# A graph attention layer: query and x rows from one product, and biases and the carried row added by VectorE

## The reference

```
q = (x @ Wq + bq); k = (x @ Wk + bk); v = (x @ Wv + bv)      # 6250 x 128, 8 heads of 16
scores = sum(q[dst] * k[src], per head) * 16**-0.5 + (edge_attr_64 @ We + be)
max_s = segment_max(scores, dst)
e = exp(scores - max_s[dst])
denom = segment_sum(e, dst) + 1e-10
probs = e / denom[dst]
agg = segment_sum(probs * v[src], dst)
out = layernorm(x + agg @ Wo + bo)                            # no scale, no shift, eps 1e-5
```

## Time and profile before

| | us |
|---|---|
| runs | 2404.39, 2408.98, 2410.76 |
| median | 2408.98 |
| the profiled execution | 2400.68 |
| its span | 2398.6 |
| PE busy | 1449.8 |
| DVE busy | 1493.1 |
| ACT busy | 526.8 |
| POOL busy | 1496.5 |

### The profile page before, as it was taken

One profiled execution on the slowest core, in us unless ns is written; L12 is line 12 of the kernel. 1 busy time (PEld: TensorE's weight loads), 2 busy tenths in 40 slices (PEclk: granted clock), 3 DMA queues, 4 the chain that ended last, 5 costly groups with the idle time before them and its releaser, 6 DMA issues.

```text
span 2398.6 us, 23254 instructions
## 1 busy us (share of the span) xinstructions
PE 1449.8 (60%) x5480; PEld 979.4 (41%) x5480; DVE 1493.1 (62%) x3591; ACT 526.8 (22%) x1868; POOL 1496.5 (62%) x1572
## 2 busy tenths in 40 slices
PE   5454576656575666565655656565756565656566
PEld 4333353434343444343433434343434343434344
DVE  3365676657566666565666657565666666657666
ACT  0121221212122222222221222122222222222211
POOL 4745546666666666666666666666666666666661
PEclk7666777867677767777787777787877677777786
DMA  6643444545455445454545455454555454545440
GB/s 230 194 111 112 111 133 145 143 144 144 134 153 151 134 125 162 124 162 128 159 131 159 126 152 135 143 145 137 150 147 140 140 146 126 162 126 161 125 126 24
DMA packets 123029, 335.73 MB, mean 140 GB/s; under 512 B 47360, under 2 KB 55301, under 8 KB 115853
## 3 DMA queue, kind: packets, MB, share of 16 engines
q0 software_dynamic: 74624, 203.26, 30.1%
q1 hardware_dynamic: 45520, 124.28, 18.7%
q10 hardware_dynamic: 2748, 6.69, 0.7%
HBM read 323.82 MB, written 10.29 MB: 139 GB/s over the span
## 4 chain that ended last, share of the span: by engine, by line
POOL 32%; another core or an unknown queue 21%; issue 19%; PE 17%; DVE 9%; ACT 2%; DMA 1%; ACTq 0%; DVEq 0%
POOL kv_buf L487 32%; PE ps_a L1191 5%; PE ps_q L1156 4%; DVE prod L787 2%; DVE wv L819 2%; PE ps_t L1156 2%; PE ps_e L1168 1%; DVE score L797 1%; PE ps_a L1234 1%; DVE x_first L807 1%; ACT x_first L559 1%; PE ps_s L1213 1%; DMA kv_buf<-kv_table,src_i 1%; PE ps_s L1219 0%
## 5 line engine op out<-in xcount | busy, mean ns | idle before, releaser
L487 POOL DMA_INDIRECT kv_buf<-kv_table,src_i x1536 | 1468.9, 956 | 842.2 <-issue 437.9
L1191 PE MATMUL ps_a<-wv,x_first 128*128 128x272 f32 x1564 | 571.8, 500 | 325.3 <-ACT wv L605 188.5
L1191 PEld LDWEIGHTS ps_a<-wv,x_first 128*128 128x128 f32 x1564 | 362.3, 242 | 497.1 <-issue 212.1
L787 DVE TENSOR_TENSOR prod<-ps_q,kv_buf 128x512 f32<-128x512 f32 x262 | 179.9, 686 | 472.2 <-remote 296.2
L1156 PE MATMUL ps_q<-q_blk,x_first 128*128 128x256 f32 x1046 | 354.7, 472 | 22.6 <-issue 22.6
L797 DVE TENSOR_REDUCE score<-prod 128x32 f32<-128x512 f32 (+1 forms) x392 | 267.3, 682 | 7.9 <-issue 0.2
L819 DVE TENSOR_TENSOR wv<-kv_buf,ps_w 128x512 f32<-128x512 f32 (+1 forms) x392 | 266.0, 678 | 1.6 <-ACT keep L597 0.2
L1156 PEld LDWEIGHTS ps_q<-q_blk,x_first 128*128 128x128 f32 x1046 | 234.6, 239 | 79.1 <-issue 40.7
L787 DVE TENSOR_TENSOR prod<-ps_t,kv_buf 128x512 f32<-128x512 f32 (+1 forms) x130 | 89.1, 685 | 225.8 <-remote 128.4
L559 ACT ACTIVATE x_first<-dst_bc,neg_node 128x256 f32<-128x256 int32 (+1 forms) x392 | 197.0, 503 | 47.8 <-DMA dst_bc<-in_dst_row 30.4
L568 ACT ACTIVATE x_first<-x_first 128x256 f32<-128x256 f32 (+1 forms) x392 | 157.8, 403 | 215.8 <-remote 193.4
(11 more groups left out here) (140 smaller groups left out, 1550.3 us busy)
## 6 DMA issues: line engine op xcount, KB each, us to landing
edge_f<-in_edge_blk SPq DMA_DIRECT2D x55, 1024.0 KB
dst_bc<-in_dst_row SPq DMA_DIRECT2D x108, 448.0 KB
kv_buf<-kv_table,src_i POOLq DMA_INDIRECT x1536
kv_table<-kv_buf ACTq DMA_DIRECT2D x12, 512.0 KB, 2.7
xt_blk<-in_x_t SPq DMA_DIRECT2D x114, 32.0 KB
out<-y_out SPq DMA_DIRECT2D x114, 32.0 KB
kv_buf<-in_x_perm SPq DMA_DIRECT2D x5, 512.0 KB, 4.2
edge_f<-in_edge_blk SPq DMA_DIRECT2D x2, 512.0 KB
```

The costliest lines, as they stand in the source:

```text
L487: pool.indirect_dma_start(kv_buf[:, b % NBUF, t, :], None, kv_table, bass.IndirectOffsetOnAxis(ap=src_i[:, column:column + 1], axis=0)).th ...
L787: dve.tensor_tensor(prod[:, q % 2, 0:n * D].rearrange("p (t d) -> p t d", d=D), ps_q[q % SPREADS][:, 0:n * D].rearrange("p (t d) -> p t d" ...
L1191: one = pe.matmul(sums(b), edge_hots[:, q % EHOT, k * P:(k + 1) * P], wv[:, q % WVBUF, 2 * k:2 * k + 2, :].rearrange("p j w -> p (j w)"), ...
```

## The change

1. The one-row product of the carried row (`sum_carry`) is removed. After `copy_halves` has copied the two halves, DVE adds the carried row to row 0 of the copy, reading both from PSUM and `carried`. `copy_halves` now waits for PE's sum itself (`s_summed`), then for its own copies and for `s_carried`; `scale_carry` waits for `s_halves` in place of `s_carrysum`.
2. `project_q` issues one product of 256 columns: x with [Wq scaled, identity] (`w_qx`). ACT's `copy_q` is removed. DVE's `add_bias` adds the biases: two operations of 64x128 write the queries, one of 128x128 writes x + bo into a new buffer `x_res` (7 blocks deep).
3. `finish_rows` issues the product with Wo alone. ACT's `copy_projected` is removed; DVE's `add_rows` adds the product and `x_res` into `y_in`.
4. `xt_blk` has 3 buffers, not 7, and its load waits for the queries (`s_newq`), not for `finish_rows`.
5. At the start DVE builds `w_qx` (a scaling and a copy of the identity), PE spreads the two biases over all partitions with two one-row products, and DVE copies them. The first three blocks' `add_bias` stands on DVE ahead of the slots; the three `copy_q` stood on ACT.

The core of the diff:

```diff
+            def add_bias(b):
+                dve.wait_ge(s_newq, b + 1)
+                if b >= QBUF:
+                    dve.wait_ge(s_byedge, FIRST[b - QBUF + 1])
+                if b >= RBUF:
+                    dve.wait_ge(s_yin, b - RBUF + 1)
+                for j in range(2):
+                    own = slice(j * W, (j + 1) * W)
+                    dve.tensor_tensor(q_blk[own, b % QBUF, j * D:(j + 1) * D], new_qx[own, 0:D], bias_qo[own, 0:D], ALU.add)
+                dve.tensor_tensor(x_res[:, b % RBUF, :], new_qx[:, D:2 * D], bias_qo[:, D:2 * D], ALU.add).then_inc(s_qcopied, 1)
+
+            def add_rows(b):
+                dve.wait_ge(s_wo, b + 1)
+                if b >= 1:
+                    dve.wait_ge(s_normal, b)
+                dve.tensor_tensor(y_in[:, :], projected(b), x_res[:, b % RBUF, :], ALU.add).then_inc(s_yin, 1)
...
             def copy_halves(b):
-                dve.wait_ge(s_carrysum, b + 1)
+                dve.wait_ge(s_summed, FIRST[b + 1])
...
-                one.then_inc(s_halves, 1)
+                one.then_inc(s_copiedhalves, 1)
+                dve.wait_ge(s_copiedhalves, b + 1)
+                if b >= 1:
+                    dve.wait_ge(s_carried, b)
+                dve.tensor_tensor(sums_sb[0:1, b % 2, :], half_sums(b, 0)[0:1, :], carried[:, :], ALU.add).then_inc(s_halves, 1)
...
+                    if chain(v, 6) is not None and chain(v, 6) + QBUF < NB:
+                        add_bias(chain(v, 6) + QBUF)
+                    if at_node(v, 5) is not None:
+                        add_rows(at_node(v, 5))
...
-                pe.matmul(sums(b)[:, 0:WV], ident[0:1, :], carried[:, :], start=False, stop=True).then_inc(s_carrysum, 1)
...
-                pe.matmul(new_q, ones[0:1, :], bias_row[:, 0:D], start=True, stop=False)
-                pe.matmul(new_q, xt_blk[:, b % XBUF, :], w_qkv[:, 0:D], start=False, stop=True).then_inc(s_newq, 1)
+                pe.matmul(new_qx, xt_blk[:, b % XBUF, :], w_qx[:, :], start=True, stop=True).then_inc(s_newq, 1)
...
-                pe.matmul(projected(b), ones[0:1, :], bias_row[:, QKV:QKV + D], start=True, stop=False)
-                pe.matmul(projected(b), xt_blk[:, b % XBUF, :], ident[:, :], start=False, stop=False)
-                pe.matmul(projected(b), agg_t[:, :], w_o[:, :], start=False, stop=True).then_inc(s_wo, 1)
+                pe.matmul(projected(b), agg_t[:, :], w_o[:, :], start=True, stop=True).then_inc(s_wo, 1)
```

More of the change, by code:

```diff
@@ L275, in graph_attention @@
         s_found = sem("s_found")
-        FOUND = numbered("spread", "falls")
+        FOUND = numbered("spread", "bias qo", "falls")
         s_spread = sem("s_spread")
@@ L577, in copy_terms @@
                                ).then_inc(s_termscopied, 1)
-            def copy_q(b):
-                act.wait_ge(s_newq, b + 1)
-                if b >= QBUF:
-                    act.wait_ge(s_byedge, FIRST[b - QBUF + 1])
-                act.copy(q_blk[0:W, b % QBUF, 0:D], new_q[0:W, :])
-                act.copy(q_blk[W:P, b % QBUF, D:2 * D], new_q[W:P, :]).then_inc(s_qcopied, 1)
             def exponentials(b):
@@ L613, in copy_turned @@
                 act.copy(agg_t[:, :], turned(b)).then_inc(s_aggcopied, 1)
-            def copy_projected(b):
-                act.wait_ge(s_wo, b + 1)
-                if b >= 1:
-                    act.wait_ge(s_normal, b)
-                act.copy(y_in[:, :], projected(b)).then_inc(s_yin, 1)
             def inverse_deviation(b):
@@ L628, in _ @@
             with act.If(general == 0):
-                for b in range(min(QBUF, NB)):
-                    copy_q(b)
                 act.wait_ge(s_node, NODE["of blocks"])
@@ L638, in _ @@
                         exponentials(chain(v, 4))
-                    if chain(v, 6) is not None and chain(v, 6) + QBUF < NB:
-                        copy_q(chain(v, 6) + QBUF)
                     if at_node(v, 4) is not None:
                         copy_turned(at_node(v, 4))
-                    if at_node(v, 5) is not None:
-                        copy_projected(at_node(v, 5))
                     if step_in(v - SLOT - LAG) is not None:
@@ L961, in _ @@
             with dve.If(general == 0):
+                dve.wait_ge(s_const, CONST["bias qo"])
+                for b in range(min(QBUF, NB)):
+                    add_bias(b)
                 for v in SLOTS:
@@ L1115, in _ @@
             pe.matmul(step_ps[:, 0:1], ones[0:1, :], step_f[:, 0:1], start=True, stop=True).then_inc(s_found, 1)
+            pe.wait_ge(s_const, CONST["scaled"])
+            pe.matmul(spread_qo[:, 0:D], ones[0:1, :], bias_row[:, 0:D], start=True, stop=True)
+            pe.matmul(spread_qo[:, D:2 * D], ones[0:1, :], bias_row[:, QKV:QKV + D], start=True, stop=True).then_inc(s_found, 1)
             def turn_first(g):
@@ L1265, in _ @@
                         sum_step(v)
-                    if at_node(v, 0) is not None:
-                        sum_carry(at_node(v, 0))
                     if chain(v, 1) is not None:
@@ L1283, in _ @@
                     pe.matmul(ps_w[:, 0:D], ones[0:1, :], bias_row[:, 0:D], start=True, stop=False)
-                    pe.matmul(ps_w[:, 0:D], xt_blk[:, 0, :], w_qkv[:, 0:D], start=False, stop=True).then_inc(e_pe, 1)
+                    pe.matmul(ps_w[:, 0:D], xt_blk[:, 0, :], w_qx[:, 0:D], start=False, stop=True).then_inc(e_pe, 1)
                     after(pe, "pe", e_act, b * len(EACT) + EACT["q copied"])
```

29 lines of the change are left out of this document (17 added, 12 removed).

## The result

| | us |
|---|---|
| before, median of 20 | 2401.8 |
| changed kernel, median of 20 | 2413.32 (2403.1 to 2431.36) |
| ratio of the two, 95% interval | 1.0049 (1.0034 to 1.0064) |
| changed kernel, the profiled execution | 2418.86, span 2416.9 |

The change made the kernel about 0.5% slower. As a change I forecast +1 us; it was +11.5.

The account below looks back on a forecast made before the run. The prediction took a queue draining gathers at some 1.4 us each as the bound. Start +3, steady blocks +2 and end -4 gave +1 us on the median 2408.98, so 2410, with 2385 to 2445 for 8 in 10.

Parts of the forecast that it names:

- No change: Whole kernel: fewer products but no time difference that a measurement can tell, the limit being 0.3%, 7.2 us; chance 42%.
- slower: Whole kernel: both sizes of the second rival together, 22% for +8 to +40 us and 10% for more; chance 32%.
- second rival: DVE's additions lie on the path from POOL's restart to its next gate: +8 to +40 us, 22%; more, 10%.
- What bounds the kernel: Steady blocks: a queue drained at some 1.4 us a gather makes 28 gathers take 40.7 us, not POOL's 35.0.
- I cost this at nothing in the steady part; the drain of the gathers hides it: PE in each block: four products fewer free 1.0 to 1.3 us of 40.7, worth no time.
- I take 0.04 us a block, 2 us in all: DVE in each block: 1.47 us of additions, almost all hidden while the queue still holds gathers; +2 us in total.
- the third pause: POOL's pause beyond each block's usual two, paid by half of the blocks; claimed to lie inside the drain.
- That the pauses stay at steps 1 and 4: POOL in each block: the period of 28 gathers in 40.7 us was to stay as before.
- The start, +3 us: Before gathers take over, DVE bounds, so its additions count in full, plus new preparations: +3 us (0 to +8).
- The end, -4 us: Last 49 us, without gathers: 5.3 us of products leave the chain, DVE's additions join it; -4 us (-5 to -2).
- The third rival: ACT without `copy_q` reaches `copy_weights` earlier, so PE's sums and POOL's restart come earlier: -11 to -28 us; chance 18%.
- Identifying the Most-Contended Engine: Optimise the busiest engine first; by it, moving work from ACT (22%) to DVE (62%) goes the wrong way; no size given.

Follow-up runs that it names:

- group 1: Follow-up kernels timed side by side with the kernel before on one chip; the kernel before took 2051.44 us there.
- carry_alone: Kernel before with only the carried row's one-row product removed and DVE adding that row in `copy_halves`; ratio to before 0.9966 in group 1.
- group 3: Follow-up kernels timed side by side with the kernel before on one chip; the kernel before took 2422.31 us there.
- group 2: Changed kernel again, and the kernel before with gathers one step further ahead, timed beside the kernel before, which took 2406.09 us there.
- group 4: Changed kernel a third time, and a version with `add_bias` one slot later, timed beside the kernel before, which took 2424.49 us there.
- products_out_2: Kernel before without its carried-row, two bias and x products, DVE given nothing and output incomplete; ratio to before 1.0030 in group 3.

## Why the prediction was right or wrong

The time lay in the range of 2385 to 2445. "No change" had been given 42% and "slower" 32%; it was slower, by an amount that lies in the first size of the second rival (+8 to +40). So the range held, and the sum inside it (+3 + 2 - 4) did not. By the steps:

- **What bounds the kernel.** Right. A step more of lead moved the pauses by one step and gained at most a little (0.9983, interval to 1.0000). In group 1, where nothing is held, a block takes 35.4 us (1591.9 / 45 for carry_alone), which is POOL's own 35.0 of the prediction's first paragraph.
- **"I cost this at nothing in the steady part; the drain of the gathers hides it" (PE's relief).** Wrong. The relief gains nothing, as I said, but it is not free where signals are held: in group 3 it costs 7.9 us by itself, with restarts at step 2 and the longest middle of its group. Its amount was mis-sized too: PE's busy time fell by 126 us, 2.2 us a block and not 1.0 to 1.3. I had priced a one-row product at the 0.33 us between two starts, where the earlier trace rows have 0.75 and 0.79 us for its two records.
- **"I take 0.04 us a block, 2 us in all" (VectorE's additions).** This term was mis-sized: the middle 45 blocks lost 17.1 us, 0.38 us a block, in the profile. Of the second rival's mechanism a part is shown. The place of the additions matters, since moving 0.87 us of them one slot gives 11 us back, and VectorE's whole load with PE full costs 20.8 us. But in group 3 this load didn't lengthen the middle, and in the restart shown above the additions stand ahead of the wait. How the 17.1 us divide between additions behind a restart and restarts moved to a worse step is not shown. My argument that the third pause lies inside the drain took the places of the restarts as given; it did not ask what a restart at step 2 would cost (1.501 us a gather).
- **That the pauses stay at steps 1 and 4.** Wrong. Many moved to 2, 5 and 6.
- **The start, +3 us.** Too small, and for the wrong reason. I priced the operations. The profiles show handshakes that are still to come when the gathers begin and then wait 4 to 11 us each: +2 us in one profile, +17 and +18 in the others, and +19 inside group 2.
- **The end, -4 us.** Right in sign: 50.6 us from the last gather to the end became 47.7, 47.3 and 50.0. In the last chain the one-row products are gone. In this part of the changed kernel's chain the product with Wo stands alone, with 0.81 us; before it had 0.43 us, with 0.79 + 0.72 ahead of it:

```profile
2385.03 0.43 PE ps_a L1246 x2
```

```profile
2403.76 0.81 PE ps_a L1259 x2
...
2408.91 0.81 PE ps_a L1259 x2
```

- **The third rival (ACT is set free).** ACT's wait for the queries is gone, but its waits turned up elsewhere: those for the landing of the edges' destinations grew from 27.0 to 70.8 us between 400 and 2200 us, and no time was gained. First before, then the changed kernel:

```profile
ACT x_first L559 <- DMA dst_bc<-in_dst_row: 27.0, 17, 2.7
```

```profile
ACT x_first L563 <- DMA dst_bc<-in_dst_row: 70.8, 22, 6.9
```

- **The Trainium skill's "Perfetto Trace Analysis", Identifying the Most-Contended Engine,** has one optimise the engine with the highest occupancy first. From it I had read that the change should lose, since it loads a fuller engine, and had set that aside because DVE's share is a mean of 62%. The change lost. The shares alone don't carry that reading, though: POOL (1496.5 us) and DVE (1493.1) are level in the page of before, and they give neither the size nor the place. In the restart shown above DVE is busy from 699.8 to 705.2 without a break, and that is the stretch that counts.

What stays open: why a lighter PE gets the restarts into another slot (it may reach one slot further before its signals are held; no run sets that apart, and the runs of 20 gathers don't tell, since the changed kernel has 19 and 16 of them in two profiles but 5 in group 4, and products_out_2 has 2), and how PE's relief and VectorE's load interact when both are timed side by side.

## What to carry to other kernels

Where a queue paces a kernel and all engines are released at once, look at the work between the release and the next gate of the queue, and at which point of the program the release falls. Average shares of busy time say little of this, and even removing work can go with releases at a worse place. So price added operations by where they stand, and measure a relief by itself before counting on it. Look at how many handshakes between engines are still to come when a long stream of transfers begins. And compare times only among kernels that were timed side by side.

## What the runs showed of the hardware

The kernel before took 2051 us in group 1 and 2402 to 2424 us everywhere else, and one chip showed both. In group 1 a gather is issued each 1.26 us and POOL hardly pauses. The window from 600 to 800 us of carry_alone in group 1, against 137 gathers in the earlier trace rows:

```profile
600.00:800.00 200.00, 127.18 (x502) 86.53 (x502) 145.35 (x359) 51.91 (x187) 151.58 (x159) 0.79 0.58 164
```

Everywhere else each gather needs some 1.45 us in the mean, and engines go on late while a run of gathers is under way: ACT waited 5.16 us for a product that PE had done 4.9 us earlier. In the middle of the run (400 to 1900 us) this wait of ACT for the projected queries has 134.7 us in 16 waits that end with something remote, the longest 12.9; in carry_alone of group 1 it has 22.8 us in 22 waits, the longest 1.7. Of DVE's 8.04 us in the earlier trace rows it can't be said that a signal was held, since the multiplication also needs its gathered rows: their last gather had begun at 1009.09, 8.2 us before it. The multiplication before it started 2.8 us after its own last gather.

In group 1's carry_alone POOL has no pause above 4 us between the first table gather and block 7, where before has five, of 6.9 to 27.5 us. The table's part is slower as well outside group 1: POOL's first table gather starts at 62.05 us in the kernel before and at 39.81 us in carry_alone of group 1:

```profile
62.05 0.94 POOL L487 DMA_INDIRECT kv_buf<-kv_table,src_i  x1 [24.22 <-DMA kv_table<-kv_buf]
```

```profile
39.81 0.95 POOL L487 DMA_INDIRECT kv_buf<-kv_table,src_i  x1 [1.87 <-DMA kv_table<-kv_buf]
```

The view of the transfers' issues has a median of 2.8 us from a gather's issue to its landing in group 1; in the traces of the others it gives no figure. What makes the difference between the groups no run here shows.

```profile
kv_buf<-kv_table,src_i POOLq DMA_INDIRECT x1536, 2.8
```
